# One set of a row's convolved inputs in place of two, with one more buffer in each of three rings

## What is computed

```python
xb = silu(conv3(xn @ W_in)[..., :512])           # a row's inputs
dt = softplus(xb @ W_dt + b_dt)
Bi, Ci = xb @ W_B, xb @ W_C                       # 16 states each
# per step t: h = exp(dt * A) * h + (dt * x) * B;  y = sum over states of h * C
y = (y + D_param * xb) * silu(z)
x1 = x + ga * (h1 + y @ W_out)
out = x1 + gb * sum_e w_e * (silu(h2 @ gate_e) * (h2 @ up_e)) @ down_e
```

## Time and profile before

| | |
|---|---|
| median of 3 runs | 2636.5 us (2634.78 to 2637.89) |
| the profiled execution | 2637.64 us, span 2635.9 us from the first to the last instruction |
| busy over the span | DVE 91%, PE 87%, POOL 86%, ACT 56% |
| drive of a unit, POOL L1361 | 512 times, mean 2790 ns |
| scan, DVE L765 | 512 times, mean 2292 ns |
| product with C, DVE L778 | 480 times, mean 1220 ns |
| decay, ACT L1133 | 1024 times, mean 681 ns |
| weighting of an expert step, POOL L1328 | 256 times, mean 1602 ns |
| DMA | 558.72 MB, POOL's queue 51.2% and SP's 36.9% of 16 engines' span |

### The profile page before, as it was taken

The page is one execution under the profiler, slowest core; times in us unless marked ns, Lnnn a source line. Parts: engine busy times, 40 slices in busy tenths (PEclk is TensorE's granted clock), DMA queues, the critical chain, the costliest instruction groups (busy, mean ns, idle before and its releaser), DMA issues.

```text
span 2635.9 us, 28145 instructions
## 1 busy us (share of the span) xinstructions
PE 2303.2 (87%) x8814; PEld 1648.3 (63%) x8814; DVE 2385.8 (91%) x2390; ACT 1489.0 (56%) x2825; POOL 2255.9 (86%) x1591
## 2 busy tenths in 40 slices
PE   6356998989989898998989899898989999898799
PEld 2224675756667576666757666575666667576678
DVE  4999999999999999999999999999999999999922
ACT  5656556565655656565565656556565665654320
POOL 2888999998999899899989998999889899988812
PEclk9677999999999999999999999999989999899899
DMA  6998999989999998989999898998989899898911
GB/s 167 256 218 209 216 224 215 235 207 243 214 219 222 210 243 200 248 215 219 222 206 248 192 246 211 224 224 207 249 193 235 209 229 233 200 249 192 233 49 48
DMA packets 312886, 558.72 MB, mean 212 GB/s; under 512 B 46864, under 2 KB 157456, under 8 KB 312736
## 3 DMA queue, kind: packets, MB, share of 16 engines
q0 software_dynamic: 77568, 260.08, 51.2%
q1 hardware_dynamic: 235168, 296.84, 36.9%
HBM read 295.10 MB, written 10.06 MB: 116 GB/s over the span
## 4 chain that ended last, share of the span: by engine, by line
PE 46%; POOL 20%; DVE 13%; issue 9%; ACT 7%; DMA 5%; SPq 0%; POOLq 0%; DVEq 0%
PE wbank L509 17%; PE mbank L521 9%; POOL unit L1361 8%; DVE hbank L765 7%; PE wbank L410 6%; DMA gsum<-unit 4%; PE wbank L451 4%; PE wbank L536 3%; POOL gsum L1375 3%; POOL act L1328 2%; ACT z L939 2%; POOL stat L1249 2%; ACT hbank L1133 2%; PE wbank L435 1%; PE wbank L471 1%
## 5 line engine op out<-in xcount | busy, mean ns | idle before, releaser
L1361 POOL TENSOR_TENSOR unit<-dtx,b_bc 128x1024 f32<-128x1024 f32 x512 | 1417.3, 2790 | 36.5 <-DVE dtx L842 27.9
L765 DVE TENSOR_TENSOR_SCAN hbank<-hbank,unit 128x1024 f32<-128x1024 f32 x512 | 1173.3, 2292 | 50.3 <-ACT hbank L1133 46.6
L1133 ACT ACTIVATE hbank<-dt,a_neg 128x512 f32<-128x512 f32 x1024 | 669.1, 681 | 241.9 <-DVE unit L778 240.0
L1375 POOL DMA_DIRECT2D gsum<-unit x480 | 560.2, 1167 | 73.1 <-DMA gsum<-unit 35.8
L778 DVE TENSOR_TENSOR unit<-hbank,c_bc 128x1024 f32<-128x1024 f32 x480 | 585.4, 1220 | 22.5
L521 PE MATMUL mbank<-down_t,act 128*128 128x256 f32 x2048 | 525.0, 394 | 27.0 <-POOL act L1328 25.9
L509 PE MATMUL wbank<-h_t,up_t 128*128 128x256 f32 x2048 | 509.9, 394 | 37.7 <-DVE xb L636 27.2
L1328 POOL TENSOR_TENSOR act<-act,w_all 128x512 f32<-128x512 f32 x256 | 410.0, 1602 | 142.0 <-DVE act L743 128.2
L509 PE MATMUL wbank<-h_t,gate_t 128*128 128x256 f32 x2048 | 487.3, 381 | 6.3 <-DVE xb L636 5.6
L521 PEld LDWEIGHTS mbank<-down_t,act 128*128 128x128 f32 x2048 | 398.7, 198 | 148.6 <-issue 51.5
L509 PEld LDWEIGHTS wbank<-h_t,up_t 128*128 128x128 f32 x2048 | 397.8, 197 | 141.3 <-DVE xb L636 38.8
(11 more groups left out here) (140 smaller groups left out, 2210.8 us busy)
## 6 DMA issues: line engine op xcount, KB each, us to landing
gsum<-unit POOLq DMA_DIRECT2D x480, 512.0 KB, 7.9
b_bc<-bc_scratch SPq DMA_DIRECT2D x352, 256.0 KB, 7.2
c_bc<-bc_scratch SPq DMA_DIRECT2D x352, 256.0 KB, 7.2
w_all<-w_scratch SPq DMA_DIRECT2D x256, 256.0 KB, 4.9
ht<-in_L_attn_x_dram SPq DMA_DIRECT2D x16, 512.0 KB, 6.1
w_out<-in_L_attn_W_out_dram SPq DMA_DIRECT2D x16, 512.0 KB, 8.0
ht<-in_L_attn_x_dram POOLq DMA_DIRECT2D x16, 512.0 KB, 8.0
out_dram<-xt SPq DMA_DIRECT2D x16, 512.0 KB, 3.1
```

What stands on the lines that cost most here:

```text
L765: eng.tensor_tensor_scan(h, h, unit[:, g % RING, :, :].rearrange("p a t -> p (a t)"), 0.0, ALU.mult, ALU.add).then_inc(scanned, 1)
L1133: eng.activation(hbank[g % HB][:, a, :], dt[:, 2 * q + a, :], ACT.Exp, scale=a_neg[:, 2 * q + a, n:n + 1]).then_inc(decayed, 1)
L1361: eng.tensor_tensor(unit[:, g % RING, :, :], dtx[:, 2 * q:2 * q + 2, :], b_bc[:, s:s + 1, :].to_broadcast([P, 2, T]), ALU.mult).then_inc(d ...
L1375: eng.dma_start(gsum[:, 2 * pair + k, :, :], unit[:, g % RING, :, :], accum_op=ALU.add).then_inc(summed[pair][k], 16)
```

## The change

`xb` goes from two sets to one (8 KB a partition less). The room goes to one more unit buffer (4 KB), one more row of B (2 KB), which is now loaded four units ahead, and one more buffer of expert weights (2 KB). AHEAD, C_RING and C_LEAD stay. In place of the wait for y of two rows before, DVE now waits, before it writes `xb` of a row, until both `dtx` pairs (`dtx_made`) and both base pairs (`base_made`) of the row before are made.

```diff
-    RING, AHEAD = 5, 2
+    RING, AHEAD = 6, 2
-    B_RING, C_RING, W_RING = 4, 4, 2
-    B_LEAD, C_LEAD = 3, 3
+    B_RING, C_RING, W_RING = 5, 4, 3
+    B_LEAD, C_LEAD = 4, 3
...
-        xb = sb("xb", [P, 2 * DK, T])
+        xb = sb("xb", [P, DK, T])
...
-        def xb_at(row, q):
-
-            return q + DK * (row % 2)
...
                     need.wait_ge(silu_act, n)
-                    if row >= 2:
-                        y = work.at["y", row - 2, q]
-                        need.wait_ge(y.full, y.after)
-                    eng.scalar_tensor_tensor(out=xb[:, xb_at(row, q), :], in0=t.bank[:, :], scalar=1.0, in1=cv, op0=ALU.add,
+                    need.wait_ge(dtx_made, 2 * row)
+                    for made in base_made:
+                        need.wait_ge(made, 2 * row)
+                    eng.scalar_tensor_tensor(out=xb[:, q, :], in0=t.bank[:, :], scalar=1.0, in1=cv, op0=ALU.add,
                                              op1=ALU.mult).then_inc(t.free, 1)
```

More of the change, by code:

```diff
@@ L409, in step_sizes @@
                     for k in range(DK):
-                        m = eng.matmul(t.bank[:, :], w_dt[:, k, m_ * P:(m_ + 1) * P], xb[:, xb_at(row, k), :],
+                        m = eng.matmul(t.bank[:, :], w_dt[:, k, m_ * P:(m_ + 1) * P], xb[:, k, :],
                                        start=k == 0, stop=k == DK - 1)
@@ L420, in rows_bc @@
                 for k in range(DK):
-                    m = eng.matmul(t.bank[0:BC, :], w_bc[:, k, :], xb[:, xb_at(row, k), :], start=k == 0,
+                    m = eng.matmul(t.bank[0:BC, :], w_bc[:, k, :], xb[:, k, :], start=k == 0,
                                    stop=k == DK - 1)
@@ L563, in product @@
                     o = t.bank[0:BC, :] if name == ("bc", 0) else t.bank[:, :]
-                    m = eng.matmul(o, w, xb[:, xb_at(0, k), :], start=k == 0, stop=k == DK - 1)
+                    m = eng.matmul(o, w, xb[:, k, :], start=k == 0, stop=k == DK - 1)
                     if k == DK - 1:
@@ L832, in first_inputs @@
                     need.wait_ge(silu_act, q + 1)
-                    eng.scalar_tensor_tensor(out=xb[:, xb_at(0, q), :], in0=t.bank[:, :], scalar=1.0, in1=first_cv[q],
+                    eng.scalar_tensor_tensor(out=xb[:, q, :], in0=t.bank[:, :], scalar=1.0, in1=first_cv[q],
                                              op0=ALU.add, op1=ALU.mult).then_inc(t.free, 1)
@@ L840, in first_steps @@
                     need.wait_ge(t.free, t.after)
-                x0 = xb_at(0, 0)
-                eng.tensor_tensor(dtx[:, 0:2, :], dt[:, 0:2, :], xb[:, x0:x0 + 2, :], ALU.mult).then_inc(dtx_made, 1)
+                eng.tensor_tensor(dtx[:, 0:2, :], dt[:, 0:2, :], xb[:, 0:2, :], ALU.mult).then_inc(dtx_made, 1)
                 need.wait_ge(dtx_made, 1)
@@ L1122, in base @@
                         need.wait_ge(y.full, y.after)
-                    eng.activation(gsum[:, 2 * pair + 1, a, :], xb[:, xb_at(row, q), :], ACT.Copy,
+                    eng.activation(gsum[:, 2 * pair + 1, a, :], xb[:, q, :], ACT.Copy,
                                    scale=d_par[:, q:q + 1]).then_inc(base_made[pair], 1)
@@ L1302, in step_sizes @@
                     need.wait_ge(driven, (row - 1) * NU + last_unit[q] + 1)
-                x0 = xb_at(row, 2 * q)
-                eng.tensor_tensor(dtx[:, pair, :], dt[:, pair, :], xb[:, x0:x0 + 2, :], ALU.mult).then_inc(dtx_made, 1)
+                eng.tensor_tensor(dtx[:, pair, :], dt[:, pair, :], xb[:, pair, :], ALU.mult).then_inc(dtx_made, 1)
                 need.wait_ge(dtx_made, 2 * row + q + 1)
```

## The result

The changed kernel takes 2660.9 us, the median of 4 runs (2658.4 to 2664.4), against 2637.2 for the kernel before in the same comparison (median of 4, 2634.8 to 2647.1). The ratio is 1.0084, 95% interval 1.0054 to 1.0113: slower by 0.84%, 24 us. The forecast was 2636.0, range 2629 to 2643, with 0.73 on no change. It was wrong, and on the side to which it gave 0.13.

What follows compares the result with a forecast made beforehand. DVE was taken to bound a slot, busy 147.48 of 153.8 us. All parts summed to 0 on 2637.64, put at the median run's 2636.5, less 0.5 for POOL's edge waits: 2636.0 us, range 2629 to 2643.

Steps and rivals of the forecast that it cites:

- The set of xb: DVE's first write of xb in a row: last readers done some 64 us earlier, so stall cost 0.
- The three waits issued there: Three more waits on VectorE's queue once a row, before writing xb: taken as 0, upper bound 12 us.
- The sixth unit buffer: POOL's wait before a drive moves about 5 us earlier: 0 on the path, between 0 and -3.6 us.
- the fifth row of B: B loaded four units ahead removes at most 3.1 us of POOL's waits; 0 on the path.
- SP's wait for the stored rows: At a slot's end it rises to some 4.6 us, the C load behind still in time by 2 us: cost 0.
- The two waits for weights: POOL's waits for expert weights, 12.9 us, at a row's first pair; not for a buffer, so they stay.
- the third buffer of expert weights: SyncE's weights loads go out one expert step earlier: gain 0, at best -1.55 us, at worst the same amount again.
- The slower rival: Earlier B and weights loads delay POOL's additions at each end of a slot: 9 us, 2645.5 us; chance 0.11.
- Its point of decision: The slower case decides from a median landing of additions of about 9.5 to 10 us.
- its cover: Time between POOL's drive ending and its scan starting, 0.6 to 2.6 us; POOL's delay reaches DVE only beyond it.
- The bound: In a middle slot of 153.8 us DVE is busy 147.48, has least idle time and sets the slot's length.
- The spread: Slots of 153.8 to 155.5 us; three such slots more or fewer out of 13 are 5 us either way.

Runs made afterwards that it cites:

- the second place alone: Kernel before with one xb set and a third weights buffer, only loads of expert steps 7 to 11 allowed one step earlier: 1.0073.
- the two held kernels: Whole change, and one xb set with only the third weights buffer; in both, B and C loads keep the weights' load's old wait: 1.0022 and 1.0057.
- the first place alone: Kernel before with one xb set and a third weights buffer, only loads of expert steps 12 to 15 allowed one step earlier: 1.0098.

## Why the prediction was wrong

**Right.** The set of xb: 0, as said, and DVE's first write of xb in a row waits for ACT, 10.0 us in 15 places, in the kernels with one set and in the kernel before alike. The three waits issued there cost nothing that can be measured (0.9996). The sixth unit buffer and the fifth row of B: 0, and POOL's waits for both are gone. SP's wait for the stored rows rose to 4.5 us at most, where 4.6 was forecast, and the load of C behind it is in time. The two waits for weights stayed at the first pair of the last two rows, and SP waits for C in place of the weights. DVE's busy time in a slot stayed at 147.5.

**The step that failed** is the third buffer of expert weights, "Gain 0; at best -1.55, at worst the same amount again". It cost 1.15% alone, some 30 us, and with the old wait put back 1.0000. The step asked who waits for weights, and found only a row's first pair, twice. It saw the 1014.2 us of SP at this load and took its end for harmless; it did not ask what stood behind it in SP's queue and with what these transfers would then share the DMA engines. In its place the runs showed two waits on POOL for a late addition, which reach PE ahead of the router and at the slot's end and lengthen the twelve middle slots by 1.5 us each.

**The slower rival** had the mechanism, with 0.11: SP set free, loads earlier, additions late. Three things in it were off. Its size: 9 us against 24. Its point of decision, a median landing of 9.5 to 10 us: the median is 7.6 and fell. Few additions count. Unit 4's went from 5.0 to 9.1 us in the mean and unit 27's from 7.1 to 8.2, while unit 6's, beside which the four loads had run before, fell from 10.5 to 5.0: the loads moved from an addition for which POOL waited 0.3 us once in the twelve slots to one for which it now waits in all twelve, 19.7 us (none before). For unit 27's it waits 13.8 us in place of 3.7. And its cover, 0.6 to 2.6 us between a drive and its scan: the damage didn't take this way. DVE waits 7.6 us for POOL's units, 4 more than before. It came by POOL's other work in the same queue, the row's mean and the weighting, to PE, and from PE to DVE. The rival looked at "the six units at each end of a slot where one pair runs alone". Both late additions lie there, but only one of the two losses does, in the end of a slot and the start of the next; the other comes out behind them, at the router.

The Trainium skill, "DMA: Bandwidth & Descriptors", section on queues, rings and completion order, says that a DMA engine takes turns between queue rows packet by packet. By that rule an addition beside loads must take longer, and the rows agree: 4.8 us before and 10.1 after, where four loads of B and C are issued from 1.5 us ahead of it to 0.7 behind it.

**The bound.** "DVE has the least idle time, so it sets the length of a slot" was read from a window of the whole slot. Cut into its eight stretches of four units, the same slot of the kernel before shows different bounds:

```profile
494.10:511.30 17.20, 17.20 (x64) 11.92 (x63) 16.73 (x14) 12.36 (x17) 14.85 (x10) 1.00 1.06 274
511.30:529.30 18.00, 18.00 (x80) 14.72 (x79) 17.30 (x15) 8.07 (x16) 17.54 (x13) 1.00 0.78 173
...
588.60:611.70 23.10, 19.84 (x70) 14.06 (x69) 22.32 (x23) 11.05 (x18) 20.16 (x14) 0.93 1.03 238
611.70:628.20 16.50, 16.50 (x59) 10.12 (x57) 16.08 (x13) 12.11 (x15) 15.50 (x12) 1.00 1.03 250
628.20:647.90 19.70, 19.70 (x80) 15.14 (x80) 18.96 (x18) 8.95 (x15) 18.00 (x13) 1.00 0.99 235
```

PE is without idle time in the first eight units and in the last eight. In the middle DVE has the least in two stretches of four (19.69 of 19.90 us in units 12 to 16, 22.32 of 23.10 in units 20 to 24), POOL in one (18.32 of 18.40 in units 16 to 20), and in units 8 to 12, where the router is, no engine is busy over 19.03 of 21.00. And the chain that ended last, on the page of the kernel before, named PE first and not DVE. Its line, and that of the changed kernel:

```profile
PE 46%; POOL 20%; DVE 13%; issue 9%; ACT 7%; DMA 5%; SPq 0%; POOLq 0%; DVEq 0%
```

```profile
POOL 29%; DVE 18%; PE 18%; issue 17%; DMA 11%; ACT 7%; POOLq 0%; SPq 0%; DVEq 0%
```

DMA went from 5% of the chain to 11%, POOL from 20% to 29%, and PE from 46% to 18%. With DVE as the only bound, PE's wait of 0.94 us for a weighted step would have cost nothing.

**The spread.** "Slots of 153.8 to 155.5 us" was read from two slots. Slots 3 to 14 of the kernel before take 153.7 to 156.6 us, those of the changed one 154.5 to 158.5. The range of 8 in 10 was built from the spread of those two; a cost of SP's order was left to the rival.

**What stays open.** Why the two places together cost less than the sum of each alone. What makes the 8.3 us ahead of slot 3 and from slot 15 on: from slot 15 on the kernels with only the unit ring or only the ring of B enlarged take 290.0 and 290.5 us, as much as the changed kernel's 290.4, and are not slower over the whole run. The third weights buffer alone has 291.0 there, and 285.9 with the old wait, so these us belong to no single ring. The twelve middle slots are surer ground, though not free of spread: the six kernels that equal the one before, it included, take 1850.1 to 1862.1 us for them, the changed kernel 1874.8, the third weights buffer alone 1878.7, but the second place alone 1863.7, only just above them. How the router's matmuls come to their clock is open too: with xb alone they take 2.96 us in the mean of these slots, more than in the changed kernel, behind the same 1.45 us of idle time as before, and the kernel is not slower. The smaller loss of the whole change against the third buffer alone (1.0084 and 1.0115, whose intervals overlap) fits with what the two held kernels show, 1.0022 and 1.0057.

No version here beats the kernel before; the best, one set of xb with the old rings, equals it and frees the room.

## What to carry to other kernels

A wait in a queue that issues in order paces everything behind it. Before a buffer is added that takes such a wait away, list the transfers that stand behind it and the ones beside which they will then run, and look at who waits for those; here a wait of 1014 us that nobody seemed to need kept 1.15% of the time. If the buffer is wanted for another reason, keep the wait: it cost 1.0000. And name the bound by stretches of a few units, not by the loop's period: a slot of which DVE is busy 96% had two quarters in which PE had no time at all.

## What the runs showed beyond that

An addition of 512 KB, with a weights' load issued 1.9 us ahead of it in both kernels, lands after 4.8 us without and after 10.1 us with four more loads of 256 KB issued around it, while the median of all 480 additions moves the other way, from 7.9 to 7.6. One weights' load of 256 KB more beside unit 27's addition makes its mean landing 8.5 us in place of 7.1. The router's sixteen matmuls take 1.93 us at best and 3.57 at worst, by the granted clock. With the first place alone PE's idle time ahead of the transposes is 2.43 us in the mean and the matmuls take 3.39; before it is 1.45 and they take 2.65. A median over the run doesn't tell this: the median of the 256 router matmuls is 263 ns before and 374 in the changed kernel, but 374 too with xb alone, which costs nothing.
